# Side matmuls spread over a state space chunk, and a convolution layer read in strips, with tokens from the first unit

## What is computed

```python
# layer 0: selective state space layer over L = 2304 pixels, 768 inner channels, 16 states
xin, z = split(xs @ in_proj_w.T)
xin = silu(causal_conv4(xin) + conv_b)
dt, Bm, Cm = split(xin @ x_proj_w.T);  dt = softplus(dt @ dt_proj_w.T + dt_proj_b)
h = exp(dt * A) * h + dt * B * xin       # for each pixel, 768 x 16
y = (h * C).sum(states) + xin * D;       out = layernorm((y * silu(z)) @ out_proj_w.T)
# layer 1: 1x1 product, filter on 8 x 8 patches in the frequency domain, 3x3 depthwise conv,
#          gelu(first half) * second half, 1x1 product
# layer 2: 11x11 depthwise convolution whose kernels are sums of 4 points
# layer 3: 4 experts, router with softmax and top 2, two 384 x 384 products per expert
```

## Time and profile before

| | us |
|---|---|
| median of three executions | 6218.57 |
| the profiled execution | 6176.16 |
| its span, first to last instruction | 6174.4 |
| VectorE busy | 4560.9 (74%) |
| TensorE busy | 5087.1 (82%) |
| ScalarE busy | 2884.5 (47%) |
| POOL busy | 2507.4 (41%) |

### The profile page before, as it was taken

How to read it: one execution, slowest core, us unless ns; L and a number is a source line. 1 busy time by engine, 2 the same in 40 slices (tenths; PEclk the granted TensorE clock), 3 DMA queues, 4 the chain that set the end, 5 groups by cost and what they waited for, 6 DMA issues and landing times.

```text
span 6174.4 us, 80875 instructions
## 1 busy us (share of the span) xinstructions
PE 5087.1 (82%) x30948; PEld 4149.2 (67%) x30948; DVE 4560.9 (74%) x5179; ACT 2884.5 (47%) x5002; POOL 2507.4 (41%) x3092
## 2 busy tenths in 40 slices
PE   5788888887888887888888877586868688999999
PEld 3666666666666666666666665365656476999998
DVE  2999999998999998999999996665565663333333
ACT  3665666665666665666666653231212222333333
POOL 3555555554555555555555543443343420000000
PEclk8999999999999999999999998687969698999999
DMA  1000000000000000000000001000001020000000
GB/s 68 1 15 25 9 9 9 9 16 24 9 9 9 9 18 22 9 9 9 9 9 9 9 5 38 27 10 22 25 14 33 8 69 19 24 31 26 29 31 20
DMA packets 74126, 115.66 MB, mean 19 GB/s; under 512 B 4708, under 2 KB 70784, under 8 KB 73740
## 3 DMA queue, kind: packets, MB, share of 16 engines
q1 hardware_dynamic: 73740, 110.48, 5.5%
HBM read 68.00 MB, written 42.47 MB: 18 GB/s over the span
## 4 chain that ended last, share of the span: by engine, by line
PE 51%; DVE 20%; issue 13%; ACT 8%; POOL 6%; DMA 0%; DVEq 0%; POOLq 0%; SPq 0%; ACTq 0%
PE pw L1621 8%; DVE a_h L707 7%; PE pw L438 6%; PE pw L430 6%; PE pw L1588 6%; DVE a_acc L722 4%; PE ps L329 3%; PE ps L389 3%; DVE b_cv L1278 3%; POOL a_xin L788 3%; PE pw L983 2%; PE ps L349 2%; PE ps L1588 2%; PE ps L1070 2%; PE pw L1070 2%
## 5 line engine op out<-in xcount | busy, mean ns | idle before, releaser
L707 DVE TENSOR_TENSOR_SCAN a_h<-a_dA,pw 128x770 f32<-128x770 f32 x1152 | 2019.7, 1753 | 293.8 <-PE pw L431 271.4
L576 ACT ACTIVATE a_dA<-a_dt,a_Aneg 128x384 f32<-128x384 f32 x2304 | 1308.3, 607 | 404.4 <-DVE a_h L707 398.9
L833 POOL TENSOR_SCALAR a_dBT<-a_dtxT,a_BC 128x768 f32<-128x768 f32 x1152 | 1039.3, 919 | 851.7 <-PE pw L431 851.7
L438 PE MATMUL pw<-g_ident,a_h 128*128 128x128 f32 x6912 | 1003.3, 282 | 416.7 <-DVE a_acc L722 410.1
L438 PEld LDWEIGHTS pw<-g_ident,a_h 128*128 128x128 f32 x6912 | 780.0, 147 | 464.7 <-DVE a_acc L722 287.3
L722 DVE SCALAR_TENSOR_TENSOR a_acc<-pw,a_BC,a_acc 128x768 f32<-128x768 f32 x1080 | 1075.6, 996 | 5.7 <-PE pw L438 5.0
L430 PEld LDWEIGHTS pw<-g_ident,a_dBT 128*128 128x128 f32 x6912 | 824.9, 142 | 235.7 <-issue 134.4
L430 PE MATMUL pw<-g_ident,a_dBT 128*128 128x128 f32 x6912 | 955.9, 275 | 5.3 <-POOL a_dBT L833 5.0
L1729 DVE TENSOR_TENSOR d_hf<-d_hf,ps 128x384 f32<-128x384 f32 x288 | 159.1, 554 | 562.2 <-ACT d_hf L1659 553.4
L788 POOL TENSOR_TENSOR a_xin<-a_xin,a_tm 128x384 f32<-128x384 f32 x432 | 433.2, 1003 | 40.7 <-POOL a_xin L788 0.9
L349 PE MATMUL ps<-a_xn,a_WinT 128*128 128x384 f32 x864 | 345.4, 502 | 66.8 <-ACT a_raw L485 60.6
(11 more groups left out here) (239 smaller groups left out, 9538.9 us busy)
## 6 DMA issues: line engine op xcount, KB each, us to landing
a_xs<-in_x SPq DMA_DIRECT2D x24, 576.0 KB, 4.0
x<-a_xs SPq DMA_DIRECT2D x24, 576.0 KB, 3.0
b_x<-x SPq DMA_DIRECT2D x24, 576.0 KB, 4.6
e_xs<-x SPq DMA_DIRECT2D x24, 576.0 KB, 3.8
out<-e_xs SPq DMA_DIRECT2D x24, 576.0 KB, 3.0
a_sx<-in_x SPq DMA_DIRECT2D x54, 192.0 KB, 2.4
x<-b_x SPq DMA_DIRECT2D x16, 576.0 KB, 3.0
x<-b_x SPq DMA_DIRECT2D x4, 936.0 KB, 3.8
```

Source lines behind the costliest of these rows:

```text
L438: t = e.transpose(m["pw2"][:, c * 128:(c + 1) * 128], m[f"a_h{g % 2}"][:, c, 1 + tb * 128:1 + (tb + 1) * 128], ident[:])
L576: e.activation(m[f"a_dA{idx // 2 % NDA}"][:, idx % 2, 1:T + 1], m[f"a_dt{k % 2}"][:, c, :], ACT.Exp, scale=m["a_Aneg"][:, c, n:n + 1]).the ...
L707: e.tensor_tensor_scan(m[f"a_h{g % 2}"][:, c:c + 2, :].rearrange("p c t -> p (c t)"), m[f"a_dA{pi % NDA}"][:].rearrange("p c t -> p (c t)" ...
L833: t = e.tensor_scalar(m[f"a_dBT{g % 2}"][:, tb, :], m[f"a_dtxT{o}"][:, tb, :], m[f"a_BC{o}"][:, tb, n:n + 1], 1.0, ALU.mult, ALU.mult)
```

## The change

- `march` takes `odd=True` in layer 0 on TensorE: side work only ahead of odd steps.
- New due times for all side work of a chunk. The input projection starts at 2.5 and has 5.4 steps per block; output products start at 14, with 2.4, 2 and 1.2 steps between; other pieces follow. POOL's `xn_pool` is at 95.
- The output products go to bank `ps2` (claim D) instead of `ps3` (claim S).
- Three strip buffers `b_xs0` to `b_xs2` of 384 pixels. For images 1 to 3, layer 1's statistics (`norm_*`) and normalisation read strips that SyncE loads from HBM (`passing`), six for each, each request waiting for the use of the strip three before. Statistics of image b+2 run at units 41 to 51 beside layer 2 of image b; those of image 1 at 30 to 40 beside layer 1 of image 0.
- Tokens at 0.5 + 1.2 n, taps from 13.6 with 10.2 units per group, output products from 26, the gates two to three units ahead of them. The image buffer is now needed only where layer 1's result is added; it is loaded at the start of the unit loop before.
- `post_*` of the last chunk is finished, with `norm_*` of image 0, before `mix_*` of image 0 begins.

```diff
@@ -82,19 +82,19 @@
 
-def march(gens, steps, main=None, scale=1.0, every=1):
+def march(gens, steps, main=None, odd=False):
 
-            if p is None or (n is not None and p.at * scale > n):
+            if p is None or (n is not None and p.at > n):
                 return
-        if n % every == 0:
+        if n % 2 or not odd:
@@ -256,6 +256,8 @@
+    for i in range(3):
+        m.new(f"b_xs{i}", [128, 3, T])
@@ -300,8 +302,11 @@
-A_AT = (7, 8, 10, 11, 13, 14)
-Z_AT = (53, 68, 71, 74, 80, 86)
+A_AT = (6.2, 7.4, 8.6, 9.8, 11, 12.2)
+O_AT, O_GAP, LN_AT = (14, 27.5, 39), (2.4, 2, 1.2), (27.6, 39.1, 46.6)
+G_AT = (60, 62.5, 66)
+T_AT = (78.6, 79.8, 81, 85.6, 86.6, 87.6)
+Z_AT = (63.5, 67.5, 71.5, 75, 82, 88.8)
@@ -321,15 +326,15 @@
-            yield 27 + 6 * tb + j
+            yield O_AT[tb] + O_GAP[tb] * j
-                S.claim("a_ob", 3 * k + tb + 1)
+                D.claim("a_ob", 3 * k + tb + 1)
-            t = e.matmul(ps[:, 0:C], m[f"a_sz{o}"][:, j, tb * 128:(tb + 1) * 128], m["a_WoT"][:, j, :], start=j == 0, stop=j == 5)
+            t = e.matmul(pd[:, 0:C], m[f"a_sz{o}"][:, j, tb * 128:(tb + 1) * 128], m["a_WoT"][:, j, :], start=j == 0, stop=j == 5)
-        yield 63 + 2 * c
+        yield G_AT[c]
@@ -341,7 +346,7 @@
-            yield 9 + 3 * i + kk
+            yield 2.5 + 5.4 * i + 1.6 * kk
@@ -349,28 +354,28 @@
-        yield 45 + j
...
@@ -452,7 +457,7 @@
-        march(side, STEPS, main, every=2)
+        march(side, STEPS, main, odd=True)
@@ -460,11 +465,11 @@
-        yield 32 + 6 * tb
+        yield O_AT[tb] + 5 * O_GAP[tb] + 0.7
-        e.activation(m["a_ob"][:, tb, :], m["ps3"][:, 0:C], ACT.Copy).then_inc(s["a_ob"], 1)
-        yield 37.5 + 6 * tb
+        e.activation(m["a_ob"][:, tb, :], m["ps2"][:, 0:C], ACT.Copy).then_inc(s["a_ob"], 1)
+        yield LN_AT[tb] + 4.3
...
@@ -772,7 +777,7 @@
-        yield 12 + 3 * i
+        yield 7.5 + 5.4 * i
@@ -798,7 +803,7 @@
-    yield 91
+    yield 95
@@ -913,15 +918,15 @@
-    return 11.5 + 0.75 * n
+    return 0.5 + 1.2 * n
-    return 20 + 8.6 * g + 0.95 * k
+    return 13.6 + 10.2 * g + 1.05 * k
-    return 29.3 + 8.6 * g + 0.4 * i
+    return 26 + 10.2 * g + 0.4 * i
@@ -961,7 +966,17 @@
-def mix_pe(e, m, w, M, b):
+NORM_AT = 41
+def norm_pe(e, m, w, M, b, at):
+    yield at + 9.3
+    M.claim("v_b1", GN * b + 24)
+    w.wait_ge("v_b1", GN * b + 23)
+    groups_pe(e, m, m["ps3"], m["b_mv0"]).then_inc(m.s["pe_gn1"], 1)
+def mix_pe(e, m, w, b):
@@ -969,10 +984,6 @@
-    yield 10.5
-    M.claim("v_b1", GN * b + 24)
-    w.wait_ge("v_b1", GN * b + 23)
-    groups_pe(e, m, m["ps3"], m["b_mv0"]).then_inc(s["pe_gn1"], 1)
@@ -1103,12 +1114,15 @@
-    march([post_pe(e, m, w, S, D, NCH - 1), mix_pe(e, m, w, S, 0)], 0)
+    march([post_pe(e, m, w, S, D, NCH - 1), norm_pe(e, m, w, S, 0, 0)], 0)
+    march([mix_pe(e, m, w, 0), norm_pe(e, m, w, S, 1, 30)], 0)
-            side += [mix_pe(e, m, w, S, b + 1), head_pe(e, m, w, S, b + 1)]
+            side += [mix_pe(e, m, w, b + 1), head_pe(e, m, w, S, b + 1)]
+        if b + 2 < NB:
+            side.append(norm_pe(e, m, w, S, b + 2, NORM_AT))
@@ -1160,10 +1174,10 @@
-            yield out_at(g, 0) - 1
+            yield out_at(g, 0) - 3.4
-            yield out_at(g, 0) - 0.9
+            yield out_at(g, 0) - 2.9
@@ -1230,27 +1245,38 @@
-def mix_dve(e, m, w, b):
-    s, dw, x, gs, sc = m.s, m["b_dw"], m[f"b_x{b % 2}"], m["b_gs0"], m["b_sc0"]
-    T1, F1, I = mix_banks(m)
-    def scale():
-        for r in range(NQ):
-            yield 4 + r
-            w.wait_ge(f"d_x{b % 2}{r}", 16 * (b // 2 + 1))
+def strip(m, b, r, again):
+    if b == 0:
+        return m["b_x0"][:, :, rows(r)], f"d_x0{r}", 16
+    j = 2 * NQ * (b - 1) + NQ * again + r
+    return m[f"b_xs{j % 3}"][:], f"d_t{j % 3}", 16 * (j // 3 + 1)
+def norm_dve(e, m, w, b, at):
+    s, gs, sc = m.s, m["b_gs0"], m["b_sc0"]
+    for r in range(NQ):
+        src, sem, value = strip(m, b, r, 0)
+        for c in range(CT):
+            yield at + 1.5 * r + 0.5 * c
+            w.wait_ge(sem, value)
-            for c in range(CT):
-                e.bn_stats(m["b_bn0"][:, c, r, :], x[:, c, rows(r)]).then_inc(s["v_b1"], 1)
-        yield 10
-        w.wait_ge("pe_gn1", b)
-        channel_dve(e, w, "v_b1", GN * b + 18, m["b_bn0"], m["b_mv0"], gs)
-        yield 10.5
-        w.wait_ge("pe_gn1", b + 1)
-        groups_dve(e, w, "v_b1", GN * b + 23, m["ps3"], gs)
-        yield 10.9
-        w.wait_ge("p_gn1", b + 1)
-        e.scalar_tensor_tensor(out=sc[:, 1, :], in0=gs[:, 1, :], scalar=-1.0, in1=sc[:, 0, :], op0=ALU.mult, op1=ALU.mult).then_inc(s["v_b1"], 1)
+            e.bn_stats(m["b_bn0"][:, c, r, :], src[:, c]).then_inc(s["v_b1"], 1)
+    yield at + 9.1
+    w.wait_ge("pe_gn1", b)
+    channel_dve(e, w, "v_b1", GN * b + 18, m["b_bn0"], m["b_mv0"], gs)
+    yield at + 9.3
+    w.wait_ge("pe_gn1", b + 1)
+    groups_dve(e, w, "v_b1", GN * b + 23, m["ps3"], gs)
+    yield at + 9.7
+    w.wait_ge("p_gn1", b + 1)
+    e.scalar_tensor_tensor(out=sc[:, 1, :], in0=gs[:, 1, :], scalar=-1.0, in1=sc[:, 0, :], op0=ALU.mult, op1=ALU.mult).then_inc(s["v_b1"], 1)
+def mix_dve(e, m, w, b):
+    s, dw, x = m.s, m["b_dw"], m[f"b_x{b % 2}"]
+    T1, F1, I = mix_banks(m)
@@ -1280,7 +1306,7 @@
-            yield out_at(g, 0) - 0.5
+            yield out_at(g, 0) - 2
@@ -1290,12 +1316,13 @@
+            w.wait_ge(f"d_x{b % 2}{r}", 16 * (b // 2 + 1))
@@ -1403,20 +1430,30 @@
-    march([post_dve(e, m, w, NCH - 1), mix_dve(e, m, w, 0), matrices_dve(e, m, w)], 0)
+    march([post_dve(e, m, w, NCH - 1), norm_dve(e, m, w, 0, 0)], 0)
+    march([mix_dve(e, m, w, 0), matrices_dve(e, m, w), norm_dve(e, m, w, 1, 30)], 0)
+        if b + 2 < NB:
+            side.append(norm_dve(e, m, w, b + 2, NORM_AT))
-def patches(t, r):
-    return t[:, rows(r)].rearrange("p (h j w) -> p j h w", j=3, w=16)
+def patches(t):
+    return t.rearrange("p (h j w) -> p j h w", j=3, w=16)
+def norm_pool(e, m, w, b, at):
+    yield at + 9.5
+    w.wait_ge("v_b1", GN * b + 27)
+    w.wait_ge("p_na", NT * b)
+    e.tensor_tensor(m["b_sc0"][:, 0, :], m["b_gs0"][:, 2, :], m["g_mhalf"][:, 0:3], ALU.pow).then_inc(m.s["p_gn1"], 1)
-    s, x, sc = m.s, m[f"b_x{b % 2}"], m["b_sc0"]
+    s, sc = m.s, m["b_sc0"]
@@ -1424,15 +1461,14 @@
-        yield 10.8
-        w.wait_ge("v_b1", GN * b + 27)
-        e.tensor_tensor(sc[:, 0, :], m["b_gs0"][:, 2, :], m["g_mhalf"][:, 0:3], ALU.pow).then_inc(s["p_gn1"], 1)
-            yield 12 if r == 0 else win_at(3 * r - 2)
+            yield 0.1 if r == 0 else win_at(3 * r - 2)
+            src, sem, value = strip(m, b, r, 1)
+            w.wait_ge(sem, value)
-                e.tensor_scalar(m[f"b_xa{r % 2}"][:, c, :].rearrange("p (j h w) -> p j h w", j=3, w=16), patches(x[:, c, :], r),
+                e.tensor_scalar(m[f"b_xa{r % 2}"][:, c, :].rearrange("p (j h w) -> p j h w", j=3, w=16), patches(src[:, c]),
@@ -1539,11 +1578,35 @@
+    def passing(b, r, again):
+        j = 2 * NQ * (b - 1) + NQ * again + r
+        if r >= 3:
+            w.wait_ge(*(("p_na", 3 * (NQ * b + r - 2)) if again else ("v_b1", GN * b + 3 * (r - 2))))
+        elif again:
+            w.wait_ge("v_b1", GN * b + 3 * (r + 4))
+        elif b > 1:
+            w.wait_ge("p_na", 3 * (NQ * (b - 1) + r + 4))
+        else:
+            l0_over(w)
+        e.dma_start(m[f"b_xs{j % 3}"][:], xv[b, :, :, rows(r)]).then_inc(s[f"d_t{j % 3}"], 16)
+    for r in range(NQ):
+        passing(1, r, 0)
+        if b + 1 < NB:
+            for r in range(NQ):
+                passing(b + 1, r, 1)
+        if 0 < b < NB - 1:
+            w.wait_ge("d_x3o", 16 * NQ * b)
+            for r in range(NQ):
+                w.wait_ge("pe_lg", NQ * (b - 1) + r + 1)
+                load(b + 1, r)
@@ -1552,15 +1615,13 @@
+            if r >= 4 and b + 2 < NB:
+                for i in range(3):
+                    passing(b + 2, 3 * (r - 4) + i, 0)
-        if b + 2 < NB:
-            w.wait_ge("d_x3o", 16 * NQ * (b + 1))
-            for r in range(NQ):
-                w.wait_ge("pe_lg", NQ * b + r + 1)
-                load(b + 2, r)
```

63 lines of the change are left out of this document (34 added, 29 removed).

## The result

The changed kernel takes 5974.64 us (median of 4 runs, 5969.44 to 5981.78), the kernel before 6212.08 in the same comparison: ratio 0.9615, 95% interval 0.9589 to 0.9641. The forecast was 5995. One execution of the kernel before, at 8479 us and a granted clock of 0.55, was in a slower state of the chip and is in no comparison.

A forecast was written before the change was run, and what follows sets the result against it. VectorE was taken to bound layer 0, with a floor of 136.5 us in each 151.15 us chunk. Layer 0 -181, handover +28 and shared stages -70 gave -223 us, 5995 us by the median; range 5870 to 6110.

The forecast's parts named there:

- Where the side matmuls stand: Layer 0, TensorE: side work between input and result transposes, spread over pairs 1 to 46, no longer delays the next scan.
- The slack of 0.7 us: Layer 0 pairs: result transposes may come about 0.7 us late before VectorE waits; later pairs stay within it, at 0.
- 2.1 and 1.5 in the sum: Idle left per layer 0 chunk: 2.1 us for crowded pairs 7 to 16, 1.5 us for POOL and evacuation waits.
- The new wait for `a_sz`: Layer 0, pair 7: TensorE's first output product waits for POOL's last `a_sz`, delaying the weighted sum 2.6 us; bounds 0, 6.
- rival 1: POOL and doubled pairs keep layer 0 slow: `a_sz` wait 6 us or more, 3 us saved per chunk; 6108 us, chance 0.12.
- Rival 3: Slower: spread work drops TensorE to 1.2 GHz in layer 0; 6495 us if 200 pairs are hit; chance 0.02.
- Saving per chunk: Layer 0: 8 us saved in each of 22 chunks, 5 more in the others, 181 us; bounds 3 to 12 per chunk.
- scan's idle before L431 down from 11.7 to about 5: Sign in layer 0: VectorE's scan waits about 5 us per chunk, mostly around pair 7, put down to `a_sz`.
- The handover: Layer 0 to image 0 of layer 1: output products done first, first token 27 us later; +28 us, bounds +10 and +45.
- The shared stages: Three stages with layer 2 beside the next image's layer 1: 23, 23 and 24 us saved, 70 us; bounds 0 and 190.
- Tokens early: 10: Shared stages: tokens from unit 0 make the first 27 units 146 us against 156, 10 us saved a stage.
- Rival 2: TensorE's clock recovers in layers 1 and 2, shared stages fall to some 260 us; 5870 us, chance 0.15.

The follow-up runs named there:

- `even`: Changed kernel with TensorE's side matmuls in layer 0 ahead of a pair's input transposes again, at the new times: 6163.1 us.
- `fill7`: Changed kernel with four extra, unread 384-column products on TensorE just ahead of its wait for `a_sz` in pair 7: 5926.8 us.
- `weave16`: Changed kernel with first output product at time 16, plus the last chunk's output products woven with image 0 again; a strip load overwrites needed data: 5852.9 us.
- `best`: `weave16` with the shared strip buffer loaded only when free, the last chunk's last three transposes at 51 to 53, image 1's statistics from 51: 5848.4 us.
- `tokonly`: Changed kernel with tokens from unit 0, but convolution, gate and output products of layer 1 at the times of before: 6098.9 us.
- `best2`: `best` with the six output products of groups 0 and 1 spaced 0.8 units instead of 0.4: 5810.2 us.

## Why the prediction was right, and where it was not

The time and the direction were right, partly because two errors had opposite signs: layer 0 gave 46 us less than forecast, layers 1 and 2 gave 22 us more. The profiled executions then differ by 200 us, where my sum was 223. The medians differ by 237, since the profiled execution of before was some 40 us quicker than its median and that of the changed kernel was not. That the forecast came within 20 us of the median is luck to that extent; from the 200 us of the traces it would have been 6018.

- **Where the side matmuls stand.** Right, and it is the larger part: `even` loses 188 us, and 7.6 us a chunk with the `a_sz` wait equal in both. The slack of 0.7 us bore the doubled pairs about as assumed: in the kernel without the `a_sz` wait all causes together leave 3.3 us of idle time a chunk, against 2.1 and 1.5 in the sum. Half of it lies in pairs from 17 on, which the sum had at 0.
- **The new wait for `a_sz`.** "Together 4.3 less 1.66: 2.6 us" is the step that failed. The wait came in the pair, from the queue and at the time that were named. But the two products and six transposes behind it were priced at full clock, and TensorE, which had just stood still for 2.6 us, ran them at half. In chunk 17 they took 4.2 us instead of 2.2, and the next steps were slow as well. The term measured 4.4 in the pair on the mean and about 5 with its tail; `fill7` gives 2.60 when the clock is held. It is inside the bound of 6 and near rival 1, whose "6 us or more" was read as POOL being late, which it was not. Rival 3 had the clock in mind, but as a level for the whole layer; it came as a short dip at pair 7, in all chunks from 3 to 21 but two, and in the chunks of 146.8 us this dip is longer and a second one follows late in the chunk.
- **Saving per chunk.** 5.6 us of idle time by the pairs instead of 8, over 22 chunks; with the wait gone it is 10.7, near the upper bound of 12. The sign "scan's idle before L431 down from 11.7 to about 5" missed: the scan has 0.6 left, and the wait is in the weighted sum, as the prediction's own sum of 2.6 had it.
- **The handover.** First token 27.6 us later against 27, image 0 longer by 2.6 against 1. Done in series it costs what the three blocks and the memset cost: in the trace 17.8 us pass from the last `a_sz` to the last block's step on POOL (forecast 20), then 6.4 for the memset and 2 for the first strip. Weaving it gave back 11 (`weave16`) and 19 (`best`) of the 30 us.
- **The shared stages.** 92 us against 70, but the split was wrong. "Tokens early: 10" is worth nothing by itself (`tokonly`: 5 to 14 us a stage slower than before the change), and the output products gave 8 to 10, where the sum had 20 for them and took 7 off for the statistics. The rest came from the convolution's start at unit 13.6 instead of 20, which I had not priced; no run has that start alone. I read TensorE's work over the whole stage; TensorE is close to full only up to unit 24, and the gain lies behind it, where the length goes with VectorE's work and waits.
- **Rival 2, the clock in layers 1 and 2.** It rose from 0.80 to between 0.85 and 0.88, not to full, and stages stayed at 275 to 300 us, not 260.
- **Strip loads and the other PSUM bank.** The first strip of a stage had 5 us in the sum: POOL waits 14.2 us for it in the stages of images 1 and 2, and TensorE 5.3 and 5.4 for POOL. The other loads and the bank were at nothing, and no wait on them is among the larger ones. Layer 3 is unchanged within 2 us.

## What to carry to other kernels

Where a change gives TensorE a new wait, look in the trace for what its clock does after a pause of that size, and price the queued work at that clock: here a 2.6 us wait cost 4.4 us in its pair and about 5 in all, and moving the waiting product one pair later paid 96 us. Where one engine paces a loop and another serves it, put side work behind the step that the pacing engine waits for next; the place within the iteration was worth 188 us, while spread work at the old place, with the new wait, ran 2 us a chunk slower than before the change. When reading waits, keep matmuls and their weight loads apart, or a pause counts twice. Before moving work in a stage, cut the stage where the mix of work changes and count each engine's work on either side.

## What the runs showed of the hardware

- Pauses of TensorE of 2.5 to 2.7 us were mostly, not always, followed by a stretch at 1.2 GHz. In the changed kernel it came in every chunk looked at (3 to 21) but 8 and 14, where the next image's statistics stand and the pause was 2.2 us; four products in the pause kept the clock at 1.00. In `even` the same pause of 2.7 us left the clock at 1.00 in chunk 3 and brought it down in chunk 4, and pair 6 took 6.5 us there and 7.9 here (windows of `even` over the two):

```profile
606.00:612.00 6.00, 4.40 (x32) 3.72 (x33) 3.34 (x3) 0.00 (x0) 4.92 (x6) 1.00 0.01 3
759.00:766.00 7.00, 5.50 (x28) 4.42 (x29) 2.91 (x3) 0.00 (x0) 4.39 (x5) 0.76 0.01 2
```

- The Trainium skill, "TensorE: Matmul & The Clock Gate", section "HAM oscillation — how this bites in real kernels", tells of a kernel whose clock falls anew at each of its waits for data. Those waits are longer than the one here. The windows around pair 7 agree in kind (1.00 ahead of the pause, 0.50 behind it); chunk 3 of `even` does not.
- The same code ran in chunks of two lengths 3.3 to 3.4 us apart (150.2 and 153.6 before, 143.5 and 146.8 after), the longer ones with more time at the lower clock. In the kernel without the `a_sz` wait the chunks away from an image's statistics were 139.9 almost without exception, and the six runs of `best2`, which has that layer 0, spread over 12 us against 55 for eleven of the kernel before in the same comparison. What decides whether a pause of 1 to 3 us brings a dip was not settled.
